# Layer 2, forward chunks 2 to 6: GpSimd multiplies two scan results by C in one instruction; its B products come a slot sooner

## The reference, cut to what matters

```python
def _selective_scan(x, dt, Bc, Cc, A, D):
    def step(h, inp):
        x_t, dt_t, B_t, C_t = inp
        dA = jnp.exp(dt_t[:, :, None] * A)
        h = h * dA + (dt_t * x_t)[:, :, None] * B_t[:, None, :]
        y = jnp.einsum('bdn,bn->bd', h, C_t)
        return (h, y)
    ...
    return ys.transpose(1, 0, 2) + x * D
# per direction: x, conv of 4 taps, silu, projections to dt, B and C, scan
y_f = _branch(x, ...)
y_b = _branch(x[:, ::-1, :], ...)[:, ::-1, :]
out = ((y_f + y_b) * silu(z)) @ W_out.T + b_out
```

## Time and profile before

| what | us |
| --- | --- |
| median of 3 runs | 19161.96 (19159.08 to 19168.01) |
| the profiled execution, its own time | 19135.61 |
| span of the profile | 19133.8 |
| one image, in the profile | about 1193, of which layer 1 about 959 |
| DVE busy | 17219.0 (90%) |
| POOL busy | 16897.2 (88%) |
| PE busy | 15370.5 (80%) |
| ACT busy | 13164.2 (69%) |

### The profile page before, as it was taken

How to read it: one execution, slowest core, us unless ns; L and a number is a source line. 1 busy time by engine, 2 the same in 40 slices (tenths; PEclk the granted TensorE clock), 3 DMA queues, 4 the chain that set the end, 5 groups by cost and what they waited for, 6 DMA issues and landing times. The chain is left out here.

```text
span 19133.8 us, 189246 instructions
## 1 busy us (share of the span) xinstructions
PE 15370.5 (80%) x45152; PEld 5349.5 (28%) x45152; DVE 17219.0 (90%) x13583; ACT 13164.2 (69%) x33157; POOL 16897.2 (88%) x11028
## 2 busy tenths in 40 slices
PE   7888878878888788887888778887788878888778
PEld 2222222222222222222222222222222222222222
DVE  7989989899898998989989899898998989989899
ACT  6767767677676776767767677676776767767676
POOL 6979979799797997979979799797997979979799
PEclk8888888888888898888888888888888988888888
DMA  2424424244242442424424244242442424424244
GB/s 73 120 61 112 119 66 118 59 113 118 68 117 60 113 117 68 117 62 115 113 68 118 65 114 109 68 120 65 113 109 68 120 66 114 107 68 120 68 116 104
DMA packets 880283, 1820.18 MB, mean 95 GB/s; under 512 B 189530, under 2 KB 594804, under 8 KB 879028
## 3 DMA queue, kind: packets, MB, share of 16 engines
q1 hardware_dynamic: 879028, 1806.77, 37.6%
HBM read 1083.46 MB, written 245.63 MB: 69 GB/s over the span
## 5 line engine op out<-in xcount | busy, mean ns | idle before, releaser
L1159 DVE TENSOR_TENSOR_SCAN arena<-ps,arena 128x897 f32<-128x897 f32 x5376 | 10985.9, 2064 | 477.9 <-ACT arena L1311 225.4
L1363 POOL TENSOR_TENSOR arena<-arena 128x896 f32<-128x896 f32 x5376 | 9417.5, 1770 | 225.5 <-DVE arena L1159 210.1
L1294 ACT ACTIVATE ps<-arena,A 128x448 f32<-128x448 f32 x10752 | 6390.8, 627 | 2400.0 <-DVE arena L1159 2318.3
L1065 PE MATMUL ps<-arena,rep 128*64 128x448 f32 x21504 | 5506.2, 642 | 1605.0 <-POOL arena L1363 1596.4
L1355 POOL TENSOR_TENSOR arena<-arena 128x896 f32<-128x896 f32 x2688 | 4772.4, 1775 | 210.0 <-DMA arena<-arena 137.5
L1065 PEld LDWEIGHTS ps<-arena,rep 128*64 128x64 f32 x21504 | 1483.1, 154 | 5247.2 <-POOL arena L1363 2835.9
L1148 DVE TENSOR_TENSOR arena<-ps,arena 128x896 f32<-128x896 f32 x2688 | 2862.7, 1065 | 75.4 <-PE ps L985 59.8
L1018 PE MATMUL ps<-arena,diag 128*128 128x448 f32 x5248 | 2193.6, 562 | 77.1 <-DVE arena L1122 77.1
L1057 PE MATMUL ps<-arena,skipd 128*128 128x448 f32 x1344 | 797.0, 679 | 711.6 <-DVE arena L1135 588.3
L1018 PEld LDWEIGHTS ps<-arena,diag 128*128 128x128 f32 x5248 | 985.3, 195 | 1265.5 <-issue 1041.7
L1344 POOL TENSOR_TENSOR arena<-arena 128x448 f32<-128x448 f32 x672 | 656.9, 982 | 512.8 <-DVE arena L1128 512.8
(11 more groups left out here) (171 smaller groups left out, 18878.1 us busy)
## 6 DMA issues: line engine op xcount, KB each, us to landing
arena<-bc_rows SPq DMA_DIRECT2D x3584, 224.0 KB, 4.6
arena<-arena SPq DMA_DIRECT2D x4160, 112.0 KB, 3.6
x_projected<-arena SPq DMA_DIRECT2D x112, 672.0 KB, 3.6
y_forward<-arena SPq DMA_DIRECT2D x112, 672.0 KB, 5.6
arena<-x_projected SPq DMA_DIRECT2D x112, 672.0 KB, 4.8
arena<-y_forward SPq DMA_DIRECT2D x112, 672.0 KB, 6.2
x<-in_x SPq DMA_DIRECT2D x119, 336.0 KB, 3.6
x_normed<-arena SPq DMA_DIRECT2D x112, 336.0 KB, 5.1
```

Of the source, the lines that this page charges most:

```text
L1065: m = e.matmul(ps[64 * h:64 * h + 64, YBANK, 0:T], rep[:, 0:64], pr[:, (q - 1 + h) % NPR, a * T:a * T + T], start=False, stop=p == NP - 1 ...
L1159: e.tensor_tensor_scan(rev(hh[:, q % NH, 0:W2], s), rev(decays(q)[:, 0:W2], s), rev(bb[:, q % NB, 0:W2], s), car[:, 2 * k + p % 2, n:n + 1 ...
L1294: e.activation(two(decays(q))[:, a, :], dt2[:, r % NR2, p % 2, :], ACT.Exp, scale=Am[s][:, 2 * k + p % 2, n:n + 1]).then_inc(c_ex, 1)
L1363: e.tensor_tensor(pr[:, q % NPR, :].rearrange("p (a b) -> p a b", a=2), two(hh[:, q % NH, :]), cr[:, p - p % 2:p - p % 2 + 2, :], ALU.mult ...
```

## The change

Five things, all in layer 1.

1. In steps 2 to 6 (`double(q)`), POOL's `output` of pairs `q` and `q + 1` is one instruction over four rows of 448 (`outputs(q)`, at even slots), C being read twice with a step of zero. It waits for `scan(q + 1)`. 120 instructions of 128x896 become 60 of 128x1792 in each image.
2. POOL's `product` is issued at slot `q - 3` instead of `q - 2`, in all steps: ahead of one more `output`.
3. Rings: NB from 3 to 4, NH from 3 to 6.
4. Due times of side jobs that prepare steps 2 to 6: all a slot sooner (`soon` 3.5 instead of 2.5), but the projection's later jobs only half a slot sooner (`u` raised by 0.5). `ye` of steps 2 to 6 a slot later.
5. `ud` is due at `t + 4.4` instead of `t + 5`, in all steps; `ys` a slot later.

```diff
-NB, NH, NPR = 3, 3, 4
+NB, NH, NPR = 4, 6, 4
+def double(q):
+    return 2 <= q // PER < NC
...
-        sp.extend([(o, "dd", i, e), (o + 0.02, "de", i, e), (t + 5 if i or e else o + 0.01, "ud", i, e)])
+        sp.extend([(o, "dd", i, e), (o + 0.02, "de", i, e), (t + 4.4 if i or e else o + 0.01, "ud", i, e)])
...
-        t = PER * (i - 1) - 2.5 * (i > 1) if i else -60
+        soon = (3.5 if i < NC else 2.5) * (i > 1)
+        t = PER * (i - 1) - soon if i else -60
...
-            project(i, t + 15.6, (1.2, 1.7, 4.7), 1.2)
+            project(i, t + 15.6, (1.7, 2.2, 5.2) if i > 1 else (1.2, 1.7, 4.7), 1.7 if i > 1 else 1.2)
...
-                act.append((t + 0.9, "ye", i, e))
+                act.append((t + (1.9 if i > 1 else 0.9), "ye", i, e))
...
+        def outputs(q):
+            r, i, k, p, s = pair(q)
+            w.wait_ge(c_sc, q + 2)
+            w.wait_ge(s_cl[p // 2], 32 * (i + 1))
+            w.wait_ge(c_sm, q - NPR + 2)
+            o, h = pr[:, q % NPR:q % NPR + 2, :], hh[:, q % NH:q % NH + 2, :]
+            e.tensor_tensor(o.rearrange("p h (a b) -> p h a b", a=2),
+                            h.rearrange("p h (a b) -> p h a b", a=2)[:, :, :, 0:T],
+                            cr[:, p:p + 2, :].unsqueeze(1).to_broadcast([128, 2, 2, T]), ALU.mult).then_inc(c_mc, 2)
...
-        for g in range(-AHEAD, Q + 1):
-            if g >= 1:
+        for g in range(-AHEAD - 1, Q + 1):
+            if g >= 1 and not double(g - 1):
                 output(g - 1)
-            if g + AHEAD < Q and not ON_VECTOR[(g + AHEAD) // NP % EJ][(g + AHEAD) % NP]:
-                product(g + AHEAD)
+            if g >= 2 and g % 2 == 0 and double(g - 1):
+                outputs(g - 2)
+            if g + AHEAD + 1 < Q and not ON_VECTOR[(g + AHEAD + 1) // NP % EJ][(g + AHEAD + 1) % NP]:
+                product(g + AHEAD + 1)
```

More of the change, by code:

```diff
@@ L128, in side_schedule @@
             project(i, t + 15.6, (1.9, 2.3, 5.2), 1.5)
-            t += 2.5
+            t += soon
             gate(i, 0, t + 21.6)
@@ L145, in side_schedule @@
         if not s:
-            sp.append((t + 1.5, "ys", i, 0))
+            sp.append((t + 2.5, "ys", i, 0))
     sp += [(PER * (NC - 2) + 13, "dg", 1, 0), (PER * (NI - 2) + 13, "dg", 0, 0)]
```

## The result

| | before | changed |
| --- | --- | --- |
| median of the runs, us | 19160.52 (4 runs) | 19509.31 (19474.8 to 19546.36, 4 runs) |
| ratio | 1 | 1.0178, interval 1.0165 to 1.0191 |
| profiled execution, us | 19135.61 | 19506.12 |

I read the changed trace by the same stretches as the earlier trace rows, again in the ninth image: layer 0, steps 0 and 1, steps 2 to 6, steps 7 to 13, then step 2 by itself and steps 3 to 6 by themselves. The columns are those of the earlier trace rows.

What follows compares the result with a forecast made beforehand. POOL was taken to pace layer 1, DVE close behind. Terms -9.7 + 1.7 + 1.5 + 0 = -6.5 us an image, x 16 = -104, took 19162 to 19058 us; 8-in-10 range 18930 to 19190.

Steps and rivals of the forecast that it cites:

- The bound: Layer 1: POOL paces it, busy 330.3 of 335.8 us in steps 2 to 6, with DVE 10 us behind.
- The wide output: POOL, steps 2 to 6: 3.295 us instead of 3.45 a pair of outputs, saving 9.3 us an image.
- Rival C: POOL's wide output takes 3.63 us, so the kernel is slower at 19298 us; chance 0.05.
- The estimate of 3.93 us: Wide output on POOL, scaled from the skill's 2.2 ns a column: 29 us an image lost; set aside for the trace.
- Steps 2 to 6: Layer 1: DVE's work 319.9 plus 6.2 idle gives 326.1 us instead of 335.8, 9.7 less an image.
- The stall at `xc`: DVE's wait for ACT's `c4` in steps 2 to 6, 9.7 us, goes because `c4` now stands ahead of `ye`.
- rival A: Steps 2 to 6: the `xc` wait moves to scans behind `ye`; no gain to tell apart, 19128 us; chance 0.17.
- The product a slot sooner: POOL's queue: no cost as work; waits of +1.7 at step 0 to 1, +1.5 at 6 to 7, 0 at backward borders.
- rival B: Step borders: from a landing of 5.6 us, POOL waits on SP's chain; slower, 19324 or 19253 us; chance 0.08.
- DVE's lead: Step borders: DVE running ahead brings `td` and SP's chain sooner, helping hold the six backward borders at 0.
- 11.8 us of cover: Loop from TensorE's sum to its dependent output: POOL has 2 wide outputs and 3 products meanwhile, so cost nothing.
- The rings: Layer 1: DVE gets about two pairs further ahead, so its pauses of 2.4 us or so no longer reach POOL.

Runs made afterwards that it cites:

- e11: The changed kernel with the spread of `du` due at t + 3.5 instead of t + 4.4: 19155.05 us, 0.9981 of the kernel before.
- e14: e2 with the spread of `du` due at t + 3.5: 19184.76 us, 1.0013 of the kernel before.
- e9: e8 with two narrow instructions in place of each wide output: 19269.07 us, 1.0046 of the kernel before.
- e2: e1 with every POOL product a slot sooner, narrow outputs and old due times: 19748.18 us, 1.0289 of the kernel before.
- e5: e1 with only the first product of each step a slot sooner: 19519.61 us, 1.0197 of the kernel before.
- e8: The changed kernel with products a slot sooner only in steps 2 to 6, where outputs are wide: 19181.96 us, 1.0019 of the kernel before.
- e3: e1 with the changed kernel's due times of side jobs: 19194.22 us, 1.0001 of the kernel before.
- e1: The kernel before with only the deeper rings, NB 4 and NH 6: 19193.18 us, 1.0000 of the kernel before.
- e13: The kernel before with only the spread of `du` due at t + 3.5: 19092.95 us, 0.9967 of the kernel before.
- e15: e11 with TensorE's `x` of the first two thirds a slot later in preparing steps 2 to 6: 19314.8 us, 1.0082 of the kernel before.
- e7: The changed kernel with all products at the old slot: 19176.22 us, 1.0021 of the kernel before.

## Why the prediction was wrong

Of the forecast's -6.5 us an image and the +21.7 that layer 1 shows in the means, the 28.2 between them lie in steps 2 to 6 (8.9), steps 0 and 1 (8.4), step 7 (2.6) and steps 8 to 13 (8.3).

**The bound** was read rightly in the main: POOL paces layer 1, and what POOL stood still for the DMA came back as time (e11, e14). Of the work taken from it in steps 2 to 6, though, only 3 to 5 of 9.3 us did (e9): DVE is that near.

**The wide output** came out as forecast. Its row:

```profile
L1378 POOL TENSOR_TENSOR arena<-arena 128x1792 f32<-128x1792 f32 x960 | 3224.1, 3358 | 132.6 <-DVE arena L1165 71.9
```

and two starts around one, POOL in step 2:

```profile
10158.28 3.37 POOL L1378 TENSOR_TENSOR arena<-arena 128x1792 f32<-128x1792 f32 x1
10161.58 1.79 POOL L1361 TENSOR_TENSOR arena<-arena 128x896 f32<-128x896 f32 x1
```

10161.58 - 10158.28 = 3.30 us, against 3.295; POOL's work in steps 2 to 6 was forecast at 321.0 and is 320.8. Rival C is excluded. The estimate of 3.93 us, scaled from the Trainium skill ("GPSIMD Engine Reference", "Elementwise — side-by-side cycle accounting"), was too high for this form.

**Steps 2 to 6** were forecast at 326.1 and took 335.1. The stall at `xc` went, as said (L1128, its wait for `c4`, is 0.0 us in this stretch). But DVE idles 16.3 us (335.1 - 318.8), not 6.2. Two groups of DVE there:

```profile
L1165 DVE TENSOR_TENSOR_SCAN arena<-ps,arena 128x897 f32<-128x897 f32 x121 | 247.0, 2069 | 10.6 <-ACT arena L1317 10.5
L1154 DVE TENSOR_TENSOR arena<-ps,arena 128x896 f32<-128x896 f32 x61 | 65.0, 1065 | 5.1 <-PE ps L991 5.1
```

This is rival A's mechanism: the wait moved from `xc` to the scans behind `ye` and to the products behind TensorE's copy of `du`. 6.87 us of it is the one stop in step 2. Steps 3 to 6 alone took 263.6 against 268.0, 4.4 less, within the 3 to 5 us that e9 gives the width. Step 2 is not a matter of the wide outputs alone: with narrow ones e2 and e5 have it at 71.7 and 72.1, and with the sooner product kept to the steps of wide outputs (e8) it is 68.6.

**The product a slot sooner** is the step that failed, as the prediction put it: "It costs nothing as work", and +1.7 at step 0 to 1, +1.5 at step 6 to 7, 0 at the backward borders, 3.2 us an image. Its stretches hold 19.3 of the 28.2 us above. Measured, with the other parts of the change beside it: steps 0 and 1 lose 10.1 (2.5 of it the new due times, by e3), step 7 loses 4.1 and steps 8 to 13 lose 8.3 in the means, 22.5 together; alone (e2 less e1) the sooner product costs 34.9. Two things were mis-sized.

- The wait itself. I had the places and the mechanism (rival B), and at step 9 forecast 0.3 us where 1.18 came; at step 0, 7.0 where 8.4 came; at the border of steps 6 and 7, 1.5 where 4.24 came, more than the upper end of 3.5. I let DVE's lead bring `td` and with it SP's chain forward. At step 9 it did not come forward: the spread is issued 4.6 us ahead of the product, where it had been 5.6.
- What a wait costs. I charged it once. The direct wait grew by 344.8 - 137.5 = 207 us, 13 us an image; layer 1 lost 21.7, with the gain of the width already in it. Pairs of kernels with one due time between them measure it more cleanly.

  From the changed kernel to e11 the direct wait fell by 16.7 us an image and layer 1 by 21.3; from e2 to e14 by 24.9 and 34.5. So a microsecond of this wait cost 1.3 to 1.4. In the kernel before, where one output more was done ahead of the wait, e13 took 5.4 us an image of it away (137.5 to 50.4) and layer 1 gave back only 2.9.

  A wait of POOL in front of an output delays TensorE's sum, by it `ye` and the decays on ACT, and by them the scans; the rows of e15 above show this chain. What POOL waits longer for beside the DMA is by the views not the scans (210.1 us before, 111.1 + 71.9 + 22.3 = 205.3 after) but TensorE, which has yet to empty `pr` (4.7 and 143.4; 121.5 of it is still there in e11, and a deeper ring `pr` was not tried).

  I had taken the loop to have 11.8 us of cover and so "cost it at nothing"; that held for the wide output by itself (e7) and not for one that starts late. Beside it, TensorE's clock fell in such a stop: in 5 us around the stop of step 2 (busy times as in the table of stretches, granted clock third from the end)

```profile
10156.20:10161.20 5.00, 5.00 (x9) 1.89 (x9) 2.06 (x2) 0.00 (x0) 5.00 (x3) 0.57 0.65 192
```

the granted clock is 0.57, near the lower of the two levels (1.2 GHz, a granted clock of 0.5), after 3.6 us in which TensorE stood still, and the eight matmuls of `x` take 6.02 instead of 3.27 us. What this adds to the total was not measured apart.

The part of rival B that failed is its condition, a landing of 5.6 us or more: from the issue of the second DMA to the start of the product it was 4.0 us at step 0, 4.3 at the border of steps 6 and 7 and 4.6 at step 9. It was enough that the issue stood in SP's queue behind loads and issues of dt that could come later, as e11 and e14 show.

**The rings** cost and bring nothing (e1). Between images the stretch without scans took 235.5 us on average instead of 233.9 (233.3 to 237.2 over all the kernels); this 1.6 us an image is not explained.

## What to carry to other kernels

When an instruction is moved ahead in an in-order queue, ask first what it waits for and what then stands behind the wait; an operand that comes by DMA has to be moved ahead on the issuing queue by at least as much, and its place there is to be read from that queue's order, not from its due time. A margin of 1.4 us in front of a move of 1.7 is no "about zero" when the waiting engine is the one that paces a ring of engines: here a microsecond of such a wait cost 1.3 to 1.4. And try the parts of a change apart: here rings and due times were worth nothing and the wide output a little, one part cost 3%, and one number on the DMA queue turned the whole into a gain.

## What the runs showed of the hardware

On GpSimd the float32 multiply `tensor_tensor` stayed on one line from 448 to 1792 columns (starts 0.94, 1.725 and 3.30 us apart), with four blocks and one operand repeated by a step of zero costing nothing extra. SP issued one DMA in 0.63 us on average here, so twelve issues ahead of the urgent one were 7.6 us, more than the 4.0 to 4.6 us from its issue to the start of the product that waited for it.
